# Compacting edge records with a 16-bit one-hot and a payload in two parts

## The reference, cut to what matters

```python
f = (e @ fc_w.T).reshape(-1, 4, 128)                 # first layer, per edge
feat = sum(leaky_relu(attn[rel] * f, 0.2), axis=1)
x = layernorm(x + segment_sum(x[src] + feat, dst))

h = x @ W.T + b                                      # second layer
e = leaky_relu(s1[src] + s2[dst], 0.01)
att = softmax of e over the edges with one src
x = layernorm(x + segment_sum(att * h[dst], src))
```

## Time and profile before

| | |
|---|---|
| median of 3 executions | 2780.12 us (2777.79 to 2781.32) |
| profiled execution | 2780.55 us, span 2778.1 us |
| edge loop within the span | about 111 to 1619 us |
| busy share, TensorE, VectorE, ScalarE, GpSimd | 82%, 85%, 55%, 72% |
| second layer and what lies between | 1624 us to the end |

### The profile page before, as it was taken

The page is one execution under the profiler, slowest core; times in us unless marked ns, Lnnn a source line. Parts: engine busy times, 40 slices in busy tenths (PEclk is TensorE's granted clock), DMA queues, the critical chain, the costliest instruction groups (busy, mean ns, idle before and its releaser), DMA issues. The chain is left out here.

```text
span 2778.1 us, 44697 instructions
## 1 busy us (share of the span) xinstructions
PE 2267.7 (82%) x11705; PEld 1447.5 (52%) x11705; DVE 2353.3 (85%) x5910; ACT 1526.3 (55%) x4524; POOL 2001.6 (72%) x1839
## 2 busy tenths in 40 slices
PE   5799999999999999999999965666566566666661
PEld 2355555555555555555555554556565566556561
DVE  7799999999999999999999985666666666666677
ACT  0266666666666666666666643444444444444442
POOL 0287787887877878788787737777777777777770
PEclk8999999999999999999999985787868876777765
DMA  3133333333333333333333333333333333333432
GB/s 93 55 98 99 97 97 96 97 97 97 99 98 98 100 97 97 96 97 97 98 99 98 90 78 79 81 80 81 80 80 80 82 80 81 80 81 81 78 75 48
DMA packets 156598, 244.05 MB, mean 88 GB/s; under 512 B 40836, under 2 KB 84398, under 8 KB 156226
## 3 DMA queue, kind: packets, MB, share of 16 engines
q0 software_dynamic: 58624, 108.72, 18.5%
q1 hardware_dynamic: 97730, 132.55, 16.7%
HBM read 231.99 MB, written 9.12 MB: 87 GB/s over the span
## 5 line engine op out<-in xcount | busy, mean ns | idle before, releaser
L501 POOL DMA_INDIRECT room<-in_x,pks x784 | 1013.4, 1293 | 353.4 <-issue 234.4
L544 POOL DMA_INDIRECT room<-h_rows,idx x832 | 785.7, 944 | 258.4 <-issue 245.6
L796 PE MATMUL FP<-fc_sb,room 128*128 128x512 f32 x1568 | 834.5, 613 | 4.6 <-DMA room<-in_e 4.6
L595 ACT ACTIVATE w_sb<-WP 128x512 f32<-128x512 f32 x784 | 468.1, 597 | 501.5 <-PE WP L805 501.5
L883 PE MATMUL FP<-ident,room 128*128 128x128 f32 x1664 | 340.1, 368 | 385.0 <-DMA room<-h_rows,idx 383.3
L805 PE MATMUL WP<-at_p,rel_oh 100*128 100x512 bf16 x2352 | 637.4, 379 | 1.8 <-ACT rel_oh L587 1.8
L883 PEld LDWEIGHTS FP<-ident,room 128*128 128x128 f32 x1664 | 288.2, 260 | 432.3 <-DMA room<-h_rows,idx 393.9
L805 PEld LDWEIGHTS WP<-at_p,rel_oh 100*128 100x128 bf16 x2352 | 228.3, 97 | 547.0 <-issue 449.2
L1110 DVE TENSOR_TENSOR z<-FP,w_sb 128x1024 f32<-128x1024 f32 x392 | 479.7, 1224 | 21.0 <-ACT w_sb L595 12.4
L680 ACT ACTIVATE accT<-accT,neg_big 128x512 f32<-128x512 bf16 x208 | 150.0, 722 | 543.1 <-DVE accT L1262 541.0
L1117 DVE SCALAR_TENSOR_TENSOR y<-z 128x2048 f32<-128x2048 f32 x196 | 447.3, 2282 | 0.0
(11 more groups left out here) (222 smaller groups left out, 2958.1 us busy)
## 6 DMA issues: line engine op xcount, KB each, us to landing
room<-in_e SPq DMA_DIRECT2D x196, 256.0 KB
rel_sb<-in_rel_g SPq DMA_DIRECT2D x196, 200.0 KB
z<-sorted_sources SPq DMA_DIRECT2D x208, 128.0 KB, 3.0
room<-h_rows,idx POOLq DMA_INDIRECT x832
room<-in_x,pks POOLq DMA_INDIRECT x784
sorted_edges<-runs,ridx POOLq DMA_INDIRECT x196
accT<-in_x_t SPq DMA_DIRECT2D x1, 3125.0 KB, 10.2
h_rows<-arena SPq DMA_DIRECT2D x13, 227.5 KB, 3.0
```

What stands on the lines that cost most here:

```text
L501: pool.indirect_dma_start(xg[:, k, u, 0:P], None, x[:, :], bass.IndirectOffsetOnAxis(ap=pks[:, k, u:u + 1], axis=0)).then_inc(xg_in[k], 16)
L544: pool.indirect_dma_start(hg[k][:, u, :], None, h_dram[:, :], bass.IndirectOffsetOnAxis(ap=idx1[:, k, u:u + 1], axis=0)).then_inc(g_in[k], 16)
L595: nc.scalar.activation(w_sb[:, u // 2, u % 2, :], WP[u % 2][:, :], ACT.Copy).then_inc(w_copied, 1)
L796: mm = pe.matmul(FP[u // 2][:, u % 2, :], e_sb[:, k, u, :], fc_sb[:, :], start=True, stop=True)
```

## The change

The payload is kept as two float16 parts, its upper bits and its lower 11 bits scaled by 1/2048. `joh` becomes float16, and a new VectorE product, `payload`, multiplies it with both parts to give `pay_oh` (64 columns). TensorE takes the bf16 `onehot` itself as weights, so `boh` and ScalarE's `blocks` go away: four products of 16-bit operands, where each float32 product was two instructions. The two halves of the result are summed by `merge` on VectorE, straight out of PSUM, in place of ScalarE's copy to `runs`. ScalarE takes over `doh`: `window_gap` writes |place - dloc| with four activations, `window` turns it to the one-hot with a Relu. The table then holds payload/2048, which the readers behind the loop scale back.

```diff
-        rank, pay = rank_pay[:, 0, :], rank_pay[:, 1, :]
+        rank = rank_pay[:, 0, :]
+        pay = rank_pay[:, 1, :].bitcast(F16).rearrange("p (c t) -> p c t", c=2)
...
-        boh = sb("boh", [P, 2, TG, NS])
-        joh = sb("joh", [P, 2, TG, J])
+        joh = sb("joh", [P, TG, J], F16)
+        pay_oh = sb("pay_oh", [P, 2, TG, 2, J], F16)
...
+            def window_gap(g, k, lead):
+
+                if not (lead and k == 0):
+                    act.wait_ge(doh_ready, g)
+                for u in range(TG):
+                    ins = nc.scalar.activation(dst_gap[:, u, :], iota_row[:, 0:W], ACT.Abs,
+                                               bias=dloc[:, bass.ds(g * TG + u, 1)], scale=-1.0)
+                ins.then_inc(dst_gap_ready, 1)
+
+            def window(g, k, lead):
+
+                act.wait_ge(dst_gap_ready, g + 1)
+                if k >= 2 or not lead:
+                    act.wait_ge(agg_done, g - 1)
+                nc.scalar.activation(doh[:, k % 2, :, :], dst_gap[:, :, :], ACT.Relu, bias=1.0,
+                                     scale=-1.0).then_inc(doh_ready, 1)
...
             def step(g, k, lead, left=SLOTS):
 
-                blocks(g, k, lead)
                 copy(g, k, lead, 0)
+                window_gap(g, k, lead)
                 copy(g, k, lead, 1)
+                window(g, k, lead)
                 if left > 1:
...
                 copy(g, k, lead, 3)
-                compact(g, k, lead)
+                places(g, k, lead)
...
-                pe.wait_ge(joh_ready, g + 1)
-                pe.wait_ge(boh_ready, g + 1)
+                pe.wait_ge(pay_ready, g + 1)
                 if not (lead and k == 0):
-                    pe.wait_ge(r_copied, 2 * g)
+                    pe.wait_ge(runs_ready, g)
                 for u in range(TG):
-                    mm = pe.matmul(EPS_T[0:NS, 0:J], boh[:, k % 2, u, :], joh[:, k % 2, u, :],
+                    member = onehot[:, :, bass.ds(g * TG + u, 1)].rearrange("p b o -> p (b o)")
+                    mm = pe.matmul(EPS_T[0:NS, 0:2 * J], member, pay_oh[:, k % 2, u, :, :].rearrange("p c w -> p (c w)"),
                                    start=(u == 0), stop=(u == TG - 1))
...
-            v.tensor_tensor(pay[:, :], t_a[:, :], t_b[:, :], ALU.add)
+            link(v.tensor_tensor(t_a[:, :], t_a[:, :], t_b[:, :], ALU.add))
+            v.tensor_scalar(t_b[:, :], t_a[:, :], (1 << PAY_BITS) - 1, None, ALU.bitwise_and)
+            link(v.tensor_scalar(t_a[:, :], t_a[:, :], PAY_BITS, None, ALU.arith_shift_right))
+            v.tensor_copy(pay[:, 0, :], t_a[:, :])
+            v.tensor_scalar(pay[:, 1, :], t_b[:, :], 1.0 / PAY_HIGH, None, ALU.mult)
...
+            def payload(g, k, lead):
+
+                dve.wait_ge(joh_ready, g + 1)
+                if not (lead and k < 2):
+                    dve.wait_ge(r_done, g - 1)
+                v.tensor_tensor(pay_oh[:, k % 2, :, :, :],
+                                joh[:, :, :].rearrange("p u (o w) -> p u o w", o=1).to_broadcast([P, TG, 2, J]),
+                                pay[:, :, bass.ds(g * TG, TG)].rearrange("p c (u o) -> p u c o", o=1)
+                                .to_broadcast([P, TG, 2, J]), ALU.mult).then_inc(pay_ready, 1)
+
+            def merge(g, k, lead):
+
+                dve.wait_ge(r_done, g + 1)
+                if not lead:
+                    dve.wait_ge(sc_in[k], PASS_SC * p + 16 + (g - k - SLOTS) * 4)
+                dve.sem_inc(dve_turn, 1)
+                v.tensor_reduce(runs[:, k, :], EPS_T[0:NS, 0:2 * J].rearrange("b (c w) -> b w c", c=2), AX.X,
+                                ALU.add).then_inc(runs_ready, 1)
...
                 records(g, k, lead)
                 weigh_pair(g, k, lead, 0)
+                payload(g, k, lead)
                 if prev:
+                    merge(*prev)
                     halve(*prev)
-                window(g, k, lead)
                 if prev:
                     finish(*prev)
                 weigh_pair(g, k, lead, 1)
```

More of the change, by code:

```diff
@@ L312, in build @@
         pass_sems = (*e_in, *rel_in, pk_ready, rel_absd, rel_ready, f_done, w_done,
-                     w_copied, z_done, y_done, hs_done, msg_ready, doh_ready, agg_done, acc_done,
-                     boh_ready, joh_ready, x_added, r_done, r_copied)
+                     w_copied, z_done, y_done, hs_done, msg_ready, doh_ready, dst_gap_ready, agg_done, acc_done,
+                     joh_ready, pay_ready, x_added, r_done, runs_ready, ridx_ready)
         pass_end = sem("pass_end")
@@ L595, in copy, with places @@
                 nc.scalar.activation(w_sb[:, u // 2, u % 2, :], WP[u % 2][:, :], ACT.Copy).then_inc(w_copied, 1)
[L597 to L609, removed]
+            def places(g, k, lead):
                 if not lead:
                     act.wait_ge(sc_in[k], PASS_SC * p + 16 + (g - k - SLOTS) * 4)
-                nc.scalar.activation(runs[:, k, :], EPS_T[0:NS, 0:J], ACT.Copy).then_inc(r_copied, 1)
-                nc.scalar.activation(ridx[:, k:k + 1], spot_i[:, bass.ds(g, 1)], ACT.Copy).then_inc(r_copied, 1)
+                nc.scalar.activation(ridx[:, k:k + 1], spot_i[:, bass.ds(g, 1)], ACT.Copy).then_inc(ridx_ready, 1)
             def step(g, k, lead, left=SLOTS):
-                blocks(g, k, lead)
                 copy(g, k, lead, 0)
+                window_gap(g, k, lead)
                 copy(g, k, lead, 1)
+                window(g, k, lead)
                 if left > 1:
@@ L656, in _ @@
                     act.wait_ge(t_turned, 1)
-                    nc.scalar.activation(both[:, 0:4 * P], EPS_T[:, :], ACT.Copy)
-                    nc.scalar.activation(both[:, 4 * P:CH * P], AP_[:, 0:(CH - 4) * P], ACT.Copy).then_inc(t_cast, 1)
+                    nc.scalar.activation(both[:, 0:4 * P], EPS_T[:, :], ACT.Copy, scale=PAY_HIGH)
+                    nc.scalar.activation(both[:, 4 * P:CH * P], AP_[:, 0:(CH - 4) * P], ACT.Copy, scale=PAY_HIGH).then_inc(t_cast, 1)
             act.wait_ge(s_dec, 1)
@@ L1075, in _ @@
             dve.sem_inc(s_pk, 1)
-            def window(g, k, lead):
-                if k >= 2 or not lead:
-                    dve.wait_ge(agg_done, g - 1)
-                v.tensor_tensor(doh[:, k % 2, :, :],
-                                iota_row[:, 0:W].rearrange("p (o w) -> p o w", o=1).to_broadcast([P, TG, W]),
-                                dloc[:, bass.ds(g * TG, TG)].rearrange("p (u o) -> p u o", o=1)
-                                .to_broadcast([P, TG, W]), ALU.is_equal).then_inc(doh_ready, 1)
             def records(g, k, lead):
-                if not (lead and k < 2):
-                    dve.wait_ge(r_done, g - 1)
-                v.tensor_tensor(joh[:, k % 2, :, :], iota_row[:, 0:J].rearrange("p (o w) -> p o w", o=1)
+                if not (lead and k == 0):
+                    dve.wait_ge(pay_ready, g)
+                v.tensor_tensor(joh[:, :, :], iota_row[:, 0:J].rearrange("p (o w) -> p o w", o=1)
                                 .to_broadcast([P, TG, J]),
@@ L1164, in _ @@
                     group(g, g % SLOTS, False)
+                merge(G0 - 1, SLOTS - 1, False)
                 halve(G0 - 1, SLOTS - 1, False)
@@ L1235, in _ @@
                     dve.wait_ge(t_sum, 1)
-                    link(v.tensor_copy(loc_i, tab_sum))
+                    link(v.tensor_scalar(loc_i, tab_sum, PAY_HIGH, None, ALU.mult))
                     link(v.tensor_scalar(loc_i, loc_i, 255, P - 1, ALU.bitwise_and, ALU.bitwise_xor))
```

18 lines of the change are left out of this document (13 added, 5 removed).

## The result

The changed kernel took 2805.27 us (median of 4 runs, 2803.88 to 2805.46) beside 2780.05 us of the kernel before on the same chip: 1.0091 times as long, 95% interval 1.0076 to 1.0106, or 25.2 us more. The forecast was 2812 us in 2786 to 2838, with 0.87 on slower. The direction, the engine and the mechanism were right. The forecast was 6.7 us too large; in the profiled executions the loop lost 22.7 us where it was to lose 29.3, which is three hundredths of a microsecond in each of its 195 steps.

What follows compares the result with a forecast made beforehand. TensorE was taken to bound the kernel at 7.63 us a group, VectorE to take over at 7.78: 0.15 x 195 = 29.3, plus 2.1 setup and 0.3 last group, 31.7 us more. Forecast 2812 us, range 2786 to 2838.

Steps and rivals of the forecast that it cites:

- The bound before: Edge loop of the kernel before: TensorE sets the step at 7.63 us, VectorE follows with 0.13 us to spare.
- `window` leaves, `payload` comes: VectorE's group: the one-hot that leaves saves 0.34 us, the new product of the same shape adds 0.34 us.
- `merge`: VectorE's group: the new reduction of 64 PSUM elements to 32 adds 0.15 us, upper end 0.30 us.
- The stall of `finish`: VectorE's group: with `window` gone, `finish` stands directly behind `halve` and waits for its result, plus 0.13 us.
- The sum: VectorE's group in the loop: 7.50 us plus the changed terms makes 7.78 us, 0.15 us over the present step.
- The setup: Ahead of the loop: four more VectorE operations and a link add 2.1 us, as VectorE works end to end there.
- ScalarE and GpSimd: In the loop: ScalarE's new work stays hidden, with 2.6 us free a group; GpSimd's group follows the step.
- Double rate for `payload`: Rival, VectorE's loop: the new product takes 0.21 us instead of 0.34, group 7.65 us, 2786 us; chance 0.08.
- More stalls: Rival, VectorE's loop: waits ahead of `merge` or its PSUM hops make the group 7.93 us, 2841 us; chance 0.15.
- The other side: Rival, loop: VectorE's group falls to 7.52 us and TensorE's saving comes through, 2761 us; chance 0.07.
- its first condition: VectorE's loop: `payload` at 0.21 us, needed together with no stall between `halve` and `finish` for 7.52 us.
- TensorE burdened by strided loads: Rival, TensorE's compaction: slow strided one-hot loads or a lower clock; group 8.1 us, 2878 us; chance 0.05.

Runs made afterwards that it cites:

- e4: Kernel before with only the destinations' one-hot (`window`) moved from VectorE to ScalarE: 2780.65 us, 1.0002 of the kernel before.
- e11: Kernel before with one more 128x256 VectorE addition a group, read by nobody, behind `window`: 2824.40 us, 1.0152 of the kernel before.
- e2: Changed kernel with `payload` multiplying `joh` by itself, all operands at step one, payload left out of the records: 3210.31 us, loop step 7.636 us.
- e5: Changed kernel with the 64-element `accumulate` of two groups before moved between `halve` and `finish`: 2786.47 us, 1.0021 of the kernel before.
- e12: Changed kernel with compaction weights packed by ScalarE, `accumulate` between `halve` and `finish`, and the records' one-hot moved to ScalarE: 1.0016 of the kernel before.
- e9: Changed kernel with ScalarE copying the four tiles' one-hot columns side by side as compaction weights: 2806.11 us, 1.0084 of the kernel before.
- e6: Kernel before with four extra unused products a group, weights 52 strided one-hot columns: 2859.07 us, 1.0278 of the kernel before.
- e7: Kernel before with four extra unused products a group, weights 52 adjacent one-hot columns: 2802.89 us, 1.0078 of the kernel before.
- e8: Kernel before with its compaction spread, one tile's part behind each tile's products, one group late: 2963.53 us, 1.0655 of the kernel before.
- e10: Changed kernel with compaction weights packed by ScalarE and `accumulate` between `halve` and `finish`: 2790.50 us, 1.0026 of the kernel before.

## Why the prediction was right, point by point

**The bound before.** TensorE sets 7.63 us and VectorE has 0.13 spare. Right: e4 takes 0.34 us from VectorE and nothing changes; e11 adds 0.34 and 0.22 come through.

**`window` leaves, `payload` comes:** -0.34 + 0.34. Measured the same; its slot is 0.33 to 0.34 us in the kernel after. e2 gives the reason: with every operand at a step of one it would hold 0.20.

**`merge`:** 0.15 forecast, 0.13 measured (1006.24 to 1006.37), the lower end of its bounds, the slot of the 64-element sum out of PSUM. Hops of 32 columns cost nothing to be seen.

**The stall of `finish`:** 0.13 forecast from the drain, 0.11 measured (1.24 against 1.13). e5 removes it and gains 18.8 us, and e12 shows the same stall behind `slope`, 0.22 us. The rule of the Trainium skill that the prediction set against this term ("VectorE: DVE Perf Modes", section "The DRAIN you can't avoid") is not what these runs show. Independent neighbours here also stand behind waits and signal semaphores, and they overlap by 0.07 to 0.09 us; what costs is to wait for the end of the instruction just ahead.

**The sum.** 7.50 + 0.13 + 0.11 = 7.74 us, and 7.744 is measured; the forecast had 7.78. In the loop 22.7 us instead of 29.3: 6.6 us too many, from two terms 0.02 us too large each. Outside the loop the profiles differ by 0.6 us where 2.4 were forecast, but the profiled execution was the shortest of the four, 1.4 us under their median; that the total misses by the same amount as the loop is partly chance. Both terms came from rows near in kind, not from the same pair in the same place.

**The setup.** 2.1 us forecast, and the four added operations do cost VectorE that: the operation behind them (`dloc`) starts 25.11 us after the engine's first in the kernel before and 27.27 after. But "works end to end" was wrong. Further on, the kernel before has two waits of VectorE for TensorE, and the one after has none there:

```profile
58.12 1.03 DVE L1054 COPY_PREDICATED y<-arena,FP 128x784 f32<-128x784 uint16 x1 [0.68 <-PE FP L779]
59.43 1.03 DVE L1054 COPY_PREDICATED z<-arena,FP 128x784 f32<-128x784 uint16 x1 [0.28 <-PE FP L779]
```

They took up 0.96 us, and 1.15 were left at the end of the setup. That the first `slope` is only 0.4 us later is also luck: VectorE began 0.33 us sooner in that execution. The first `slope` lies between 125.4 and 127.3 us in the six profiles with the old setup and between 126.2 and 130.2 in the eight with the new one.

**TensorE.** Its compaction was put at 0.25 to 0.50 us and holds 0.51, with a step of 7.63 (e2), so it was not lightened. The upper bound came out nearly right by a wrong price: the strided load was read as 124 ns from a float32 row and takes 190. What failed is the place of its wait. I wrote that it runs ahead until the compaction waits for `payload`, with 0.2 to 0.4 us idle a group and 93 to 97% busy. It waits for `add_x` ahead of the aggregate, 0.1 us a group by the starts of its products, and its busy row stays at 400.00. With no lighter compaction there was no more to wait: 7.744 us against its own 7.636. A busy row under 100% needed a TensorE that is really lighter, as in e9 (393.90).

**ScalarE and GpSimd** were rightly hidden: e4 gives ScalarE the new work with no effect, and GpSimd's row is 321.37 us of 400 beside 320.18.

**The rivals.** Double rate for `payload` (0.08) is excluded by the slot of 0.34 us; e2 shows that the mechanism exists and needs another operand. More stalls (0.15): no gap ahead of `merge`. The other side, TensorE's saving comes through (0.07): e2 reaches 7.636 us and no less, so its first condition alone gives a draw. TensorE burdened by strided loads (0.05): the loads are slow, 190 ns, but e9 shows that they have no part in the time. (That rival's sum, 0.5 x 195 + 2, is 99.5 us and not 98.)

No version ran faster than the kernel before; of those that keep the changed compaction, e12 and e5 came closest, 1.0016 and 1.0021 times its time.

## What to carry to other kernels

When two engines stand within 2% of each other, sum the slots from start to start on each, and count as instructions also the waits that a neighbour covers: an instruction that separates a producer from its consumer is worth its own time less the stall that it hides, and moving it away gains only the difference (0.34 us went, 0.11 came back; 0.21 went, 0.22 came back). Refill such a place with work whose result nobody needs soon; put there an instruction that frees another engine's buffer, and the two engines may form a ring slower than either. And count weight loads by how their columns lie, not only by their number.

## What the runs showed of the hardware

- Two VectorE instructions of which the second must wait for the first: 1.24 us from start to start against 1.13 (kernel after and e5, 128x1024 f32), 2.42 against 2.20 (e12 and the kernel after, 128x2048 f32, buffer to be overwritten).
- A load of 52 bf16 columns as weights: 190 ns with columns 1568 bytes apart, 105 ns adjacent; four such products, where TensorE sets the step, cost 0.396 and 0.115 us (e6, e7).
- A 128x256 product of 16-bit operands: 0.20 us with a step of one everywhere, 0.34 with one operand that repeats each element 32 times (e2, kernel after).
- Going from 512-column products to the compaction and back cost TensorE 0.19 us, 0.09 ahead and 0.10 behind, whether the compaction was two instructions or eight (kernel before, e8).
- `slope` took 2.32 to 2.33 us where a gather started within 0.01 us of it, 2.28 to 2.29 where the gather started 0.03 us or more ahead (e5, e10, kernel after).
